# Maxima and exponentials of two score groups in one instruction over two PSUM banks

## What is computed

```python
scores = jnp.einsum('blhd,bmhd->bhlm', q * scale, k)
attn = jax.nn.softmax(scores, axis=-1)
o = jnp.einsum('bhlm,bmhd->blhd', attn, v).reshape(b, l, c)
```

## Time and profile before

| | us |
|---|---|
| median of 3 runs (449.86 to 451.69) | 450.28 |
| the profiled execution, its own time | 449.79 |
| its span | 448.0 |
| TensorE busy | 386.4 |
| DVE busy | 333.3 |
| ACT busy | 239.5 |
| POOL busy | 187.4 |

### The profile page before, as it was taken

One profiled execution on the slowest core, in us unless ns is written; L12 is line 12 of the kernel. 1 busy time (PEld: TensorE's weight loads), 2 busy tenths in 40 slices (PEclk: granted clock), 3 DMA queues, 4 the chain that ended last, 5 costly groups with the idle time before them and its releaser, 6 DMA issues.

```text
span 448.0 us, 11399 instructions
## 1 busy us (share of the span) xinstructions
PE 386.4 (86%) x3762; PEld 278.4 (62%) x3762; DVE 333.3 (74%) x1578; ACT 239.5 (53%) x491; POOL 187.4 (42%) x576
## 2 busy tenths in 40 slices
PE   1099989999998866979999999999998989899746
PEld 0089977133895633647777776777676666667534
DVE  2899999999994435585877786777898989887120
ACT  1051010621235133466887978797787878786631
POOL 7435433344643612044354353534364636351340
PEclk9999995555555555696999999999999999999988
DMA  5445600000088000000000000000000000000000
GB/s 202 153 149 160 194 2 1 0 1 2 4 158 230 2 1 0 1 3 2 1 2 1 3 2 1 3 2 2 1 3 3 2 2 1 2 16 1 15 13 15
DMA packets 9499, 15.23 MB, mean 34 GB/s; under 512 B 1329, under 2 KB 7892, under 8 KB 9297
## 3 DMA queue, kind: packets, MB, share of 16 engines
q1 hardware_dynamic: 9442, 14.51, 11.3%
HBM read 13.88 MB, written 0.62 MB: 32 GB/s over the span
## 4 chain that ended last, share of the span: by engine, by line
PE 50%; DVE 15%; issue 11%; POOL 9%; ACT 9%; DMA 4%; SPq 1%; POOLq 0%; ACTq 0%; DVEq 0%
PE ps L775 42%; DVE nmax L1392 5%; DMA skw_r<-in_skw 4%; PE ps L978 4%; ACT skw_r L659 2%; PE ps L1035 2%; ACT brief L620 2%; ACT L651 1%; DVE st L1304 1%; POOL x L485 1%; PE ps L926 1%; ACT skw_t L634 1%; POOL tailp L460 1%; POOL tailp L458 1%; POOL tail L457 1%
## 5 line engine op out<-in xcount | busy, mean ns | idle before, releaser
L1392 DVE TENSOR_REDUCE nmax<-ps 128x4 f32<-128x512 f32 x96 | 62.6, 684 | 31.9 <-PE ps L775 31.8
L634 ACT ACTIVATE skw_t<-ps 128x512 f32<-128x512 f32 x96 | 53.4, 595 | 21.1 <-PE ps L775 20.8
L398 POOL TENSOR_TENSOR root<-grow,half 32x1 f32<-32x1 f32 x64 | 34.5, 539 | 70.2 <-DVE grow L1175 70.2
L775 PE MATMUL ps<-skw_r 54*128 54x128 bf16 x768 | 48.1, 223 | 5.9 <-DVE nmax L1392 4.0
L775 PEld LDWEIGHTS ps<-skw_r 54*128 54x128 bf16 x768 | 29.9, 96 | 27.3 <-issue 18.7
L775 PE MATMUL ps<-mT_t,fc1w_t 128*128 128x256 f32 x120 | 39.4, 420 | 1.4 <-ACT mT_t L672 1.3
L470 POOL TENSOR_TENSOR rstd<-vare,nhalf 128x1 f32<-128x1 f32 x24 | 13.3, 553 | 63.4 <-DVE vare L1310 46.8
L775 PE MATMUL ps<-fc2w,skw_r 128*128 128x144 f32 (+1 forms) x240 | 34.2, 290 | 0.6 <-ACT skw_r L659 0.6
L627 ACT ACTIVATE skw_r<-ps 128x512 bf16<-128x512 bf16 x48 | 26.1, 594 | 14.8 <-PE ps L978 14.4
L775 PE MATMUL ps<-s_t,skw_t 128*128 128x8 f32 x64 | 19.0, 371 | 16.9 <-DMA skw_r<-in_skw 16.9
L978 PE MATMUL ps<-identb,brief 128*128 128x128 bf16 x384 | 28.7, 234 | 4.9 <-DVE brief L1379 4.7
(11 more groups left out here) (222 smaller groups left out, 980.3 us busy)
## 6 DMA issues: line engine op xcount, KB each, us to landing
gmod<-spread_mods SPq DMA_DIRECT2D x3, 1408.0 KB, 9.2
skw_t<-in_skw SPq DMA_DIRECT2D x1, 2048.0 KB
adaw_t<-in_ada SPq DMA_DIRECT2D x3, 432.0 KB
tails<-in_tail SPq DMA_DIRECT2D x3, 427.1 KB
fc1w_t<-in_fc SPq DMA_DIRECT2D x3, 320.0 KB
fc2w<-in_fc SPq DMA_DIRECT2D x3, 288.0 KB
qkvw_t<-in_qkv SPq DMA_DIRECT2D x3, 216.0 KB
x<-in_x SPq DMA_DIRECT2D x1, 576.0 KB, 9.2
```

The costliest lines, as they stand in the source:

```text
L398: g.tensor_tensor(root[:, j:j + 1], grow[:, j % 4, j:j + 1], half[:], ALU.pow).then_inc(root_ready, 1)
L634: a.activation(prob[g].rearrange("p i t -> p (i t)"), ps[:, 2 + g % 2, :], ACT.Exp, scale=SCALE).then_inc(prob_ready, 1)
L775: return pe.matmul(o, lhsT, rhs, start=start, stop=stop, skip_group_check=True)
L1392: d.tensor_reduce(nmax[:, v % 2, first:first + 7:2], ps[:, 6 + g % 2, :].rearrange("p (i t) -> p i t", i=4), AX_X, ALU.max, negate=True).t ...
```

## The change

maxima(v, g) now reads banks 6 and 7 in one reduction (128x1024 to 128x8), and exps(v, g) banks 2 and 3 in one activation (128x1024). Both wait for the second group of the pair, count one increment per pair, and are called with g = 0 and g = 2 only. The waits of TensorE and of max_parts are recounted. Since there is one call for two, the lists of ACT and DVE are changed at the places where something stood between the two. The whole diff:

```diff
--- before.py
+++ after.py
@@ -628,10 +628,10 @@
                                  ps[:, 7, :].bitcast(BF16)[:, n * T:(n + 4) * T], ACT.Copy).then_inc(kT_ready, 1)
 
             def exps(v, g):
-                act.wait_ge(sT_full, 4 * v + g + 1)
+                act.wait_ge(sT_full, 4 * v + g + 2)
                 if v >= 1:
-                    act.wait_ge(prob_used, 4 * (v - 1) + g + 1)
-                a.activation(prob[g].rearrange("p i t -> p (i t)"), ps[:, 2 + g % 2, :], ACT.Exp,
+                    act.wait_ge(prob_used, 4 * (v - 1) + g + 2)
+                a.activation(skw_t[:, g * 4 * T:(g + 2) * 4 * T], ps[:, 2:4, :].rearrange("p s n -> p (s n)"), ACT.Exp,
                              scale=SCALE).then_inc(prob_ready, 1)
 
             def o_out(v):
@@ -703,12 +703,10 @@
                 if v + 1 < VISITS:
                     h_out(v + 1)
                 if slot % 2 == 0:
-                    if old:
-                        exps(w, 0)
                     if 0 < v < VISITS:
                         v_out(v)
                     if old:
-                        exps(w, 1)
+                        exps(w, 0)
                     if new:
                         k_out(v)
                     if third:
@@ -721,7 +719,6 @@
                         first(v + 1, 0)
                     if old:
                         exps(w, 2)
-                        exps(w, 3)
                     if coming and not third:
                         first(v + 1, 1)
                     if m_fc1 is not None:
@@ -991,7 +986,7 @@
             def scores(v, g):
                 pe.wait_ge(qT_ready, 2 * v + g // 2 + 1)
                 pe.wait_ge(kT_ready, 2 * v + g // 2 + 1)
-                banks = [refill(6 + gg % 2, max_ready, 4 * v + gg + 1) for gg in (g, g + 1)]
+                banks = [refill(6 + gg % 2, max_ready, 2 * v + g // 2 + 1) for gg in (g, g + 1)]
                 for n in range(4):
                     for gg in (g, g + 1):
                         _, (q, k) = operands(v, gg, n)
@@ -1006,7 +1001,7 @@
 
             def scores_T(v, g):
 
-                banks = [refill(2 + gg % 2, prob_ready, 4 * v + gg + 1) for gg in (g, g + 1)]
+                banks = [refill(2 + gg % 2, prob_ready, 2 * v + g // 2 + 1) for gg in (g, g + 1)]
                 if g == 0:
                     pe.wait_ge(nmT_ready, v + 1)
                 for n in range(4):
@@ -1023,7 +1018,8 @@
                 if g == 0:
                     refill(4, o_raw_ready, v + 1)
                     pe.wait_ge(v_ready, v + 1)
-                pe.wait_ge(prob_ready, 4 * v + g + 1)
+                if g % 2 == 0:
+                    pe.wait_ge(prob_ready, 2 * v + g // 2 + 1)
                 for n in range(4):
                     i = mm(ps[32 * n:32 * n + 32, 4, g * T:(g + 1) * T], v_aug[v % 3][:, head_of(g, n), :], prob[g][:, n, :])
                 i.then_inc(prob_used, 1)
@@ -1387,15 +1383,15 @@
                                   ps[:, 6, :].bitcast(BF16)[:, n * T:(n + 4) * T]).then_inc(qT_ready, 1)
 
             def maxima(v, g):
-                dve.wait_ge(s_full, 4 * v + g + 1)
-                first = head_of(g, 0)
-                d.tensor_reduce(nmax[:, v % 2, first:first + 7:2], ps[:, 6 + g % 2, :].rearrange("p (i t) -> p i t", i=4),
-                                AX_X, ALU.max, negate=True).then_inc(max_ready, 1)
+                dve.wait_ge(s_full, 4 * v + g + 2)
+                d.tensor_reduce(nmax[:, v % 2, 4 * g:4 * g + 8].rearrange("p (i s) -> p s i", s=2),
+                                ps[:, 6:8, :].rearrange("p s (i t) -> p s i t", i=4), AX_X, ALU.max,
+                                negate=True).then_inc(max_ready, 1)
 
             def max_parts(v):
 
                 h = v % 2
-                dve.wait_ge(max_ready, 4 * v + 4)
+                dve.wait_ge(max_ready, 2 * v + 2)
                 if v >= 2:
                     dve.wait_ge(mT_full, v - 1)
                 by_half = nmax[:, h, :].rearrange("p (n s) -> p s n", s=2)
@@ -1491,7 +1487,6 @@
                         norms(v + 1)
                     if new:
                         maxima(v, 0)
-                        maxima(v, 1)
                     if 0 <= u < VISITS:
                         gated(u)
                     if v + 2 < VISITS:
@@ -1500,7 +1495,6 @@
                         unit_parts(v + 1)
                     if new:
                         maxima(v, 2)
-                        maxima(v, 3)
                         max_parts(v)
                     if v + 1 < VISITS:
                         split(v + 1)
@@ -1513,24 +1507,18 @@
                         q_out(v)
                     if v + 2 < VISITS:
                         next_normal(v + 2)
-                    if new:
+                    if third:
                         maxima(v, 0)
-                    if third:
-                        maxima(v, 1)
                     if 0 <= u < VISITS:
                         gated(u)
                     if third:
                         norms(v + 1)
                     elif new:
-                        maxima(v, 1)
-                    if third:
-                        maxima(v, 2)
+                        maxima(v, 0)
                     if m_norm is not None:
                         second_input(m_norm)
-                    if new and not third:
+                    if new:
                         maxima(v, 2)
-                    if new:
-                        maxima(v, 3)
                     if third:
                         unit_parts(v + 1)
                     if new:
```

## The result

The changed kernel takes 455.35 us (median of 4 runs, 453.58 to 456.0), the kernel before 450.07 us beside it (449.59 to 451.69). The ratio is 1.0105, with an interval of 1.0064 to 1.0145: slower by 1%. The profiled execution took 455.94 us, its span is 453.6 us. Ratios, and medians at like clock, leave out executions more than 1.5% above the fastest of the same kernel, which are four of the 29 of before that stand beside the first four experiments.

What follows compares the result with a forecast made beforehand. TensorE was taken as the full engine (19.66 of 20 us). Terms 2.3 + 0.9 + 0.4 - 0.3 - 0.5 - 0.2 = +2.6 us gave 452.9 us against the median; own range 451.2 to 454.6, wide range 449.4 to 456.0.

Steps and rivals of the forecast that it cites:

- rival of dearer reads over two banks: Fused instructions cost more than thought, up to 1.37 and 1.19 us; 458.6 us at the end, half-way 455.7; chance 0.12.
- Prices: One fused reduction on DVE takes 1.21 us, one fused exponential on ACT 0.99 us.
- The row: Profile row of two adjacent reductions, 1.29 us: fusing a pair saves 0.07 us, 3.4 us of DVE over 48 pairs.
- Odd slots 5 to 13: Gated now precedes the fused reduction, so TensorE starts the second scores 0.45 us later; 5 x 0.46 = 2.3 us lost.
- I count no recovery: Odd slots 5 to 13: TensorE's later 0.24 us wait for POOL absorbs nothing, since that chain slips by the same 0.45.
- rival of the absorbed stall: TensorE's late start of the second scores is made up before the slot pair ends; not slower, 450.8 us; chance 0.20.
- Slots 3 and 23: Same list as slots 5 to 13: second scores start later, 2 x 0.46 = 0.9 us lost.
- Slots 15 and 17: pv waits for the fused exponential, so the next scores come 0.19 us later; 0.4 us lost for two slots.
- Slots 19 and 21: The slip of pv is covered and DVE's two pairs give back 0.07 us each; 2 x 0.14 = 0.3 us saved.
- Even slots: Slots 6 to 22: exponentials 2/3 stand ahead of table load and gelu, which frees h_turn's bank; 9 x 0.06 = 0.5 us saved.
- Opening slots 0 to 2: Five pairs of maxima on the chain, each 0.07 us shorter and 0.03 later; 0.2 us saved.
- The sum: All terms together add 2.6 us: 452.4 us from the profiled execution, 452.9 against the median, 0.6% more.

Runs made afterwards that it cites:

- one_wait: The change, but the scores of a pair wait once instead of twice for the count of the fused reduction; ratio to before 1.0082.
- max_first: The change, but in odd slots of layers 1 and 2 the fused reduction of pair 0/1 stands ahead of gated; ratio to before 1.0030.
- best: max_first with one wait for the maxima, single exponentials of groups 0 and 1 in slots 15 to 21 (odd), single reductions around gated in slot 23; ratio to before 1.0006.
- max_only: The change with only the maxima fused and the exponentials one per group as before; 453.22 us against 450.37, ratio to before 1.0078.
- exp_only: The change with only the exponentials fused, the maxima and DVE's list as before; ratio to before 1.0039.
- order_only: The kernel before with DVE's list in the order of the change and nothing fused; ratio to before 1.0101.

## Why the prediction came out as it did

The direction, the mechanism and the place were right, and 455.35 us lies inside 449.4 to 456.0. The forecast's own 452.9 was too low: 455.35 lies outside the 451.2 to 454.6 that it gave itself. It lies in the wide range only because that was kept open upwards for the rival of dearer reads over two banks, whose half-way time was 455.7; that rival is refuted below, so the number fell into the range by luck. By its steps:

- **Prices.** The fused reduction was to take 1.21 us and takes 1.220; the fused exponential 0.99 and takes 1.022. Both bounds held, and the rival of dearer reads over two banks falls. The prediction set against it the rule of the Trainium skill (VectorE: DVE Perf Modes, the section on the TRN2 errata), by which a large tile pays the fixed latency once. That section speaks of instructions that read SBUF, while these read PSUM; the prediction passed over that. Taken as the prediction took it, the busy time of the maxima would fall by 7.5 us. It fell by 4.1, from 62.6 to 58.5, where the overlap of neighbours is counted once, and a pair that stood together shrank from 1.28 to 1.22. The row decided rightly.
- **Odd slots 5 to 13.** 2.3 us were predicted and 2.88 came, with a period of 20.89 us for the 20.7 expected. The wait of TensorE is there in each (0.51 us), with the reduction as releaser (of the nine waits in the view, those of slots 0, 1 and 3 were there before, so six are new, with slot 23's); the mis-sized term is the release, the time from the end of the reduction to TensorE's start: 0.26 us instead of the 0.14 that slot 3 showed. one_wait shows why: both waits of the pair now ask for one count. The step that took 0.14 from a row in which the first wait was already met was the error. It left 0.58 a slot for 0.46.
- **"I count no recovery"** held: 0.24 us of TensorE's wait for POOL before, 0.24 after, and even slots add 0.00. The rival of the absorbed stall falls.
- **Slots 3 and 23.** 0.9 us were predicted. Slot 23 added 0.58 and slot 24 gave back 0.22. Slot 3 added 0.38 and slot 4 gave back 0.30. But max_first and best have nearly the same pair of numbers there (+0.42 and -0.39, +0.42 and -0.31), so slot 3's share is not that of this wait. TensorE's mean granted clock from 200 to 205 and from 205 to 210 us was 0.65 and 0.67 in before, 0.87 and 0.50 in the change, so a stretch at the lower level lies differently across these slots. That alone does not explain the pair of numbers: max_only has 0.66 in both stretches, nearly as before, and still +0.38 and -0.35. Slot 3's own cost stays open.
- **Slots 15 and 17.** 0.4 us predicted, 0.49 came, by the step as written; pv waited 1.01 us (0.95 was said). best, with single exponentials there, takes it away.
- **Slots 19 and 21.** 0.3 us predicted, -0.30 came for these two, and slots 18, 20 and 22 gave a further 0.25. max_only alone has -0.45 and exp_only -0.25 in the stretch, and order_only, which fuses nothing, -0.24: part of it is second_input's earlier place.
- **Even slots.** 0.5 us were to be saved by ACT; slots 6 to 14 gave 0.03 in all. gelu does come earlier against TensorE, but gelu(m, 1) behind it waits for fc1. In slot 8 of the change, the last fc1 matmul of its group ends at 259.04 and gelu (L659) starts at 259.14; before it was the same 0.10 us, from 255.42 to 255.52:

```profile
258.77 0.27 PE L770 MATMUL ps<-mT_u,tailw 102*128 102x256 bf16 x1
```

```profile
258.54 0.57 ACT L641 ACTIVATE skw_t<-ps 128x512 f32<-128x512 f32 x1
259.14 0.60 ACT L659 ACTIVATE skw_r<-ps 128x512 f32<-128x512 f32 x1
```

  The prediction named what stood behind the exponentials and not what else it waits for.
- **Opening slots 0 to 2.** 0.2 us were to be saved; the trace has -0.27 up to slot 3, in slots whose length differs by more than that between kernels.
- **The sum.** +2.6 predicted for the loop, +3.00 in the trace. It is that near because misses cancel: 0.6 us too little for slots 5 to 13 and 0.5 of saving in the even slots that did not come, against 0.5 too much for slots 3 and 23 with the slots behind them, and 0.25 more saved in slots 18 to 22. The rest of the measured 5.28 us is not in the loop.

**What the sum did not hold.** The profiled executions differ by 6.15 us: 3.00 in the loop, 2.65 ahead of it, 0.55 outside the span, -0.05 behind slot 25. Of the 2.65, 2.07 stand in one stretch. The timeline of TensorE in before, at 62 us:

```profile
61.99 1.14 PE L775 MATMUL ps<-bmat 64*64 64x64 f32 x16 [0.69 <-ACT bmat L554]
63.06 0.39 PE L775 MATMUL ps<-s_t,adaw_t 128*128 128x8 f32 x2
```

and in the change:

```profile
62.57 1.97 PE L770 MATMUL ps<-bmat 64*64 64x64 f32 x16 [0.69 <-ACT bmat L554]
64.47 0.59 PE L770 MATMUL ps<-s_t,adaw_t 128*128 128x8 f32 x2
```

The same matmuls take 1.14 us in the one and 1.97 in the other, 0.39 and 0.59. I read that as the two levels of TensorE's clock, 2.4 and 1.2 GHz, though the granted clock does not say so by itself. In the windows view of 60 to 70 and 70 to 150 us (the clock is the third number from the end), before has

```profile
60.00:70.00 10.00, 9.31 (x74) 8.66 (x68) 10.00 (x88) 1.18 (x2) 3.23 (x6) 0.75 0.01 2
70.00:150.00 80.00, 78.00 (x370) 45.76 (x370) 68.44 (x479) 26.89 (x41) 35.46 (x84) 0.50 0.24 56
```

and the change

```profile
60.00:70.00 10.00, 9.31 (x71) 8.71 (x70) 10.00 (x88) 1.18 (x2) 3.22 (x6) 1.00 0.01 2
70.00:150.00 80.00, 78.00 (x368) 45.64 (x368) 66.94 (x479) 26.86 (x41) 33.40 (x76) 1.00 0.23 55
```

In before, the matmuls with 8 columns go from 0.39 to 0.59 us where the granted clock falls to 0.50, at 64.9 us. In the change they take 0.59 under a recorded 1.00. So the record of the change holds no fall, and its durations are those of the lower level all the same: here the durations have to be believed, and a higher mean of the granted clock goes with the longer opening. It is so in all nine traces. In the five with a mean of 0.97 the loop begins 2.10 to 2.65 us later than in before, in the three others with 0.85 it begins 0.50 to 1.11 later. The remaining 0.58 us of the change is the load of skw, which took 19.71 us instead of 19.14, so that the first matmuls on it start at 24.05 us instead of 23.48.

So a run's mean granted clock shows which opening it had. Of the 25 counted runs of before beside the first four experiments, 15 had 0.85 to 0.86 and a median of 449.38 us, 10 had 0.97 or more and 451.05. Three of the four runs of the change had 0.97 (455.94 us at the median), one had 0.855 (453.58). That is 4.9 and 4.2 us over before at like clock, on chips that need not be the same, against 3.0 to 3.2 in the loop. max_only and order_only, which cost 2.80 and 3.07 from slot 5 on, stand 3.4 and 3.8 us over before in the runs at 0.97, and 3.6 and 4.1 in those at 0.85. What is left over, some 1 to 2 us for the change, is open. A part may be a further spread that the mean clock does not show: of the 15 runs of before at 0.85, seven took 445.3 to 447.3 us and eight 449.4 to 450.8, and of max_only's eight, two took 449.1 and 450.2 and the other six 452.6 to 453.5. No trace here is of such a short run, so what makes it short stays open too.

## What to carry to other kernels

When two instructions become one, look at what stood between them, and at what each of the two released: here the order that came with fusing cost 2.65 us in slots 5 to 14 where nothing was fused at all, and the fused reduction in a better place cost 0.03 there. The second instruction of an adjacent pair is already cheap (0.60 us of 0.68), so fusing gives back 0.07 us a pair, and in this kernel only where that engine holds the chain. When two waits that were met one after the other turn into two for the same count, make them one: here the double wait delayed TensorE by 0.12 us each time.

## What the runs showed of the hardware

- A read of 1024 fp32 elements over two neighbouring PSUM banks costs as one stream: 1220 ns on DVE and 1022 ns on ACT, against 684 and 595 for 512. The second half costs 1.05 ns an element on DVE, and 0.83 on ACT, where the earlier trace rows had given 0.77.
- TensorE started 0.14 to 0.15 us after the end of the releasing reduction when one wait was open, 0.25 to 0.30 us after it when two waits for the same count were open (the change, max_only and max_first), and 0.14 to 0.15 again when the second was taken out (one_wait and best).
- Equal matmuls near 62 us took 1.14 us in some profiled executions (before, max_only, exp_only, best) and 1.96 to 1.97 in the others, and the loop began up to 2.65 us later in these. The recorded granted clock points the other way: its mean is 0.85 where the short matmuls were and the fall to 0.50 was recorded, and 0.97 where the matmuls were long and no fall was recorded. The runs of one kernel have both means, so a profile of before and one of a change may sit on different sides of it; comparing stretches behind it, here from slot 5 on, removes this.
